# Four extra 64-column products in each score tile of two batches of a decoder layer

## The chip, the cores and the metric

The kernel runs on one core of one Trainium2 chip. The time is the device time of one execution in microseconds (us), the median of several runs. TensorE multiplies matrices, VectorE and ScalarE work element by element, GpSimd does the slower element work and the scattered stores, and SyncE issues most transfers.

## What is computed

One decoder layer over 8 batches of 256 tokens with 128 channels, all in fp32: an attention in which each token looks at 96 chosen keys, a retention over a context, and a mixture of eight experts, each followed by a layer norm. The change lies in the attention. Its core is, cut down:

```python
I = where(local, inf, index_scores); I = where(causal, -inf, I)
_, idx = top_k(I, 96)                      # 64 near keys and 32 far ones
key, value = gathered by idx
scores = (q_c . key_c + q_r . key_r) * scale
attn = softmax(scores)
out = (attn . value) @ W_out
```

## The kernel before

Each batch goes through four stages. Stage a makes queries, keys and the list of far keys; stage b is the attention; stage c the attention's output, the retention and two norms; stage d the router. A last part, the tiles of 128 sorted token rows, runs the experts. The five engines run one program each. `program` writes all of them in the same order: in step n, batch n is in stage b, batch n+1 in stage a, batch n-1 in stage c, batch n-2 in stage d, and each step has `NS` = 20 slots. Expert tiles fill some slots, at the earliest from step 2 on, so the steps of batches 0 and 1 have none. An engine takes its instructions in the order written; semaphores carry the waits between engines.

Stage b takes a batch in `NT` = 16 score tiles of 16 tokens and 8 heads (128 rows). Tiles 0 to 3 (before `T0`) look at near keys alone, the other twelve at far ones too. In slot s TensorE does this, and the text calls it a round:

- `scores(s)`: the products of tile s into bank bS (lines 988 to 994). They wait for VectorE or ScalarE to be done with bS, and the far part for `gs`.
- `gather(s+1)`: one to three 512-column products into bank bG with a one-hot matrix, which pick the far keys of the next tile (line 975). VectorE turns bG into `gs` (line 1668).
- some products of stages a and c, and of the experts.
- behind a wait for `m_out` (ScalarE has emptied bank bM): `weigh(s-2)`, small products of probabilities and values (lines 1018 and 1023), `far_latents(s)`, four small transposes, and `turn(s-1)`, which waits for `s_nrm` and transposes the normed probabilities `ppn` of tile s-1 (line 830, bM<-cst,ppn: two 128-column products in tiles from 4 on, one before).

Beside it VectorE takes the maximum of the scores (`nmx`), divides (`rls`, `ppn`), makes `gs`, and does stage a's search for the largest index scores; ScalarE does the exponential (`pp`) and copies bM into `pts`, `vgs` and `ots`.

Bank bM has 512 columns of 4 bytes: transposed probabilities at 0 to 255, far values at `LATENT` = 256, weighed values at `WEIGHED` = 384 to 447. Columns 448 to 511 are not used in stage b. `ident` is a 128x128 identity held in `cst`; in `MM(out, stationary, moving)` the second argument is loaded into the array and the third streams through.

Of the kernel before, what the change touches and what calls it, by code (L numbers as in the profile page):

```python
# [35 lines left out]
NT = L // TQ  # L36
# [7 lines left out]
SCORES_AT = (5.5, 6, 7, 8, 9.5, 10.5, 11.5, 12.5)  # L44
LEAD_A, LEAD_C, LEAD_D = 2, 2, 4
FIRST_C = -4


def most_tiles(batches):
# [164 lines left out]
def build(nc, io, out):  # L214
    ctx = ExitStack()
    with ctx:
# [124 lines left out]
        bG, bS = pb("bG"), pb("bS")  # L341

        bM = pb("bM")
        TURNED, LATENT, WEIGHED = 0, 256, 384
        bW = [pb("bW0"), pb("bW1")]
        bC = pb("bC")
        bH = pb("bH")
# [79 lines left out]
        def program(stage_a, stage_b, stage_c, stage_d, tile_list, tile, collect, summed, means, normed, dense, dense_end):  # L427

            listed = {GROUPS[g][0][-1] + 2: g for g in range(len(GROUPS))}
            for step in range(-2, NB + 1):  # L430
# [4 lines left out]
                for s in range(NS):  # L435
                    def run(f, at_, k, lead, low=0):

                        for own, i in ((at_ + lead, batch(k)), (at_ + lead - NS, batch(k + 1))):
                            if i is not None and own >= low:
                                if own == low:  # L440
                                    f(low - 1, i)
                                f(own, i)
# [5 lines left out]
                    run(stage_a, s, 1, LEAD_A)  # L448
                    run(stage_c, s, -1, LEAD_C, FIRST_C)
                    run(stage_b, s, 0, 0)  # L450
# [3 lines left out]
                    run(stage_a, s + 0.5, 1, LEAD_A)  # L454
                    run(stage_c, s + 0.5, -1, LEAD_C, FIRST_C)
                    run(stage_d, s + 0.5, -2, LEAD_D)
# [187 lines left out]
        def _(pool):  # L644
# [88 lines left out]
            def stage_c(s, i):  # L733
                oc.batch(-1 if s < FIRST_C else 0, i.n)
                if s == FIRST_C:
                    pool.wait_ge(d_cx[i.par].sem, d_cx[i.par].at(i.half, 32))

                    pool.wait_ge(c_full.sem, c_full.at(i.n - 1, C_AT["state"] + 1))

                    pool.wait_ge(r_q.sem, r_q.at(i.n - 1, 1))  # L740
                    rotate(rkn[:, :, :], cn[:, i.par, :, :], "cos_k", "sin_k", r1, r2, r_k)
                if s == 0:

                    pool.wait_ge(c_av.sem, c_av.at(i.n - 1, 2))
                    pool.sem_inc(s_pass.sem, 1)
                    heads = lambda ap: ap.rearrange("p t (g v e) -> p t g v e", v=4, e=RD)
                    for v in range(4):
                        nc.gpsimd.tensor_copy(heads(cnm[:, :, v, :])[:, :, :, v, :],
                                              heads(cn[:, i.par, :, :])[:, :, :, v, :]).then_inc(r_v.sem, 1)
                if s == 3:  # L750
                    pool.wait_ge(c_x1.sem, c_x1.at(i.n, 1))
                    pool.wait_ge(r_k.sem, r_k.at(i.n, 1))
                    rotate(rqn[:, :, :], x1[:, :, :], "cos_q", "sin_q", r1, r2, r_q)
# [68 lines left out]
        def _(pe):  # L822
            for s_ in (a_full, g_full, s_full, m_full, c_full, c_av, r_full):
                pe.sem_inc(s_.sem, s_.per * s_.lead)
            MM = nc.tensor.matmul
            ident = C("ident")

            def flip(dst, src, n, lo=0):

                return MM(dst, src, ident[lo:lo + n, lo:lo + n], is_transpose=True, start=True, stop=True)  # L830
# [13 lines left out]
            for h in range(NH):  # L844
                lo = 64 * (h % 2)
                last = MM((bM, bC)[h % 2][0:CQ, 32 * (h // 2):32 * (h // 2) + 32], wuqT[lo:lo + 64, h // 2, :], wukvT[lo:lo + 64, h // 2, :],
                          start=True, stop=True)
# [131 lines left out]
            def scores(i, tile):  # L979
                p, g = i.par, tile - T0  # L980
                if tile == 0 or tile > T0:
                    pe.wait_ge(s_max.sem, s_max.at(i.n, tile))
                else:
                    pe.wait_ge(s_exp.sem, s_exp.at(i.n, tile))
                o = 0
                q = qall[:, p, 128 * tile:128 * tile + 128]
                if tile < T0:
                    MM(bS[:, o:o + 96], q, kd[:, p, 0:96], start=True, stop=True).then_inc(s_full.sem, 1)
                    return
                k0 = 32 * ((tile - T0) // 2)  # L990
                MM(bS[:, o:o + 96], q, kd[:, p, k0:k0 + 96], start=True, stop=True, skip_group_check=True)  # L991
                pe.wait_ge(g_out.sem, g_out.at(i.n, g + 1))
                for c in range(4):
                    last = MM(bS[32 * c:32 * c + 32, o + 96:o + SW], qall[0:96, p, 128 * tile + 32 * c:128 * tile + 32 * c + 32],  # L994
                              gs[:, g % 2, 128 * c:128 * c + 128], start=True, stop=True, skip_group_check=True)
                last.then_inc(s_full.sem, 1)

            def far_latents(i, tile):
                g = tile - T0
                for c in range(4):  # L1000
                    o = LATENT + 32 * c
                    flip(bM[:, o:o + 32], gs[0:32, g % 2, 128 * c:128 * c + 128], 32)

            def turn(i, tile):

                pe.wait_ge(s_nrm.sem, s_nrm.at(i.n, tile + 1))
                w = ppn[:, tile % 2, :]
                if tile < T0:
                    return flip(bM[0:96, 0:128], w[:, 0:96], 128)
                flip(bM[:, 0:128], w[:, 0:128], 128)  # L1010
                return flip(bM[:, 128:256], w[:, 96:SW], 128)
# [17 lines left out]
            def stage_b(s, i):  # L1029
                if s < 0:  # L1030
                    return
                if s == 0:
                    pe.wait_ge(a_free.sem, a_free.at(i.n, 15))
                if s == int(s):
                    if s < NT:
                        scores(i, s)
                    if T0 <= s + 1 < NT:
                        gather(i, s + 1)
                    return
                if s > int(s) + 0.25:  # L1040
                    return
                s = int(s)
                if 1 <= s <= NT + 1:
                    pe.wait_ge(m_out.sem, m_out.at(i.n, s - 1))
                    pe.sem_inc(s_pass.sem, 1)
                    if 2 <= s:
                        last = weigh(i, s - 2)
                    if T0 <= s < NT:
                        far_latents(i, s)
                    if s <= NT:  # L1050
                        last = turn(i, s - 1)
                    last.then_inc(m_full.sem, 1)
# [210 lines left out]
            def normed(n):  # L1263
                pass

            program(stage_a, stage_b, stage_c, stage_d, tile_list, tile, collect, summed, means, normed, dense, dense_end)


        @block.scalar
        def _(act):  # L1270
# [144 lines left out]
            def stage_c(s, i):  # L1415
                full = lambda use: act.wait_ge(c_full.sem, c_full.at(i.n, C_AT[use] + 1))
                free = lambda ins: ins.then_inc(c_freeA.sem, 1)
                oc.batch(-1 if s < FIRST_C else 0, i.n)
                if s == 1:
# [87 lines left out]
        def _(dve):  # L1507
# [189 lines left out]
            def stage_c(s, i):  # L1697
# [4 lines left out]
                two = lambda ap: ap.rearrange("p (t c) -> p t c", t=2)  # L1702
                oc.batch(-1 if s < FIRST_C else 0, i.n)
                if s == -2.5:
# [242 lines left out]
```

## Time and profile before

| | |
|---|---|
| runs of before | 773.82, 762.03, 766.42 us; median 766.42 |
| profiled execution | 757.35 us, of which the span from the first to the last instruction is 755.5 |
| instructions | 18822, on TensorE 6549 products and as many weight loads |
| busy, share of the span | TensorE 85%, its weight loads 66%, VectorE 63%, ScalarE 49%, GpSimd 36% |
| mean granted TensorE clock | 0.868 of full speed |

In the profile PE is TensorE's product, PEld its weight load, DVE VectorE, ACT ScalarE, POOL GpSimd. An fp32 product that is no transpose leaves two PE records and two PEld records, a transpose one of each. "128*96 128x512" is a stationary operand of 128 rows and 96 columns and a moving one of 128 rows and 512 columns. PEclk is the clock that was granted to TensorE, as a share of 2.4 GHz: it is either 1.00 or 0.50, and a value between them is a stretch that holds both. Products are pipelined, so that the duration of one record is longer than the time until the next one starts, and a busy share of 100% is not full use. A span of "us" in the timeline covers all records of its row ("x8").

### The profile page before, as it was taken

The page shows a single profiled execution, that of the slowest core. Times are in us where ns is not written, and L with a number is a line of the kernel's source. Part 1 is how long each engine was busy: PE and PEld are TensorE (multiplying, and loading weights), DVE is VectorE, ACT ScalarE, POOL GpSimd, SP SyncE. Part 2 cuts the span into 40 slices and gives each one's busy share as a digit, 9 for nine tenths or more (in the row PEclk, how much of TensorE's full clock was granted, in tenths as well). Part 3 has the DMA queues.
Part 4 walks back from the last instruction along what each step waited for, and adds up shares of the span by engine and source line. Part 5 has one row for each costly group of instructions (what it writes and reads, how often), then busy time and mean ns, then how long its engine had stood idle before and what let it go on. Part 6 is the DMA issues. An engine that isn't in the chain of part 4 may idle for free.

```text
span 755.5 us, 18822 instructions
## 1 busy us (share of the span) xinstructions
PE 644.0 (85%) x6549; PEld 495.8 (66%) x6549; DVE 473.1 (63%) x1733; ACT 369.5 (49%) x1271; POOL 274.7 (36%) x451
## 2 busy tenths in 40 slices
PE   5469988997999899988998999889977997567794
PEld 4245664675577677755686777757766776457794
DVE  1618647876985797578766975687744674314334
ACT  4335445453565476544554766355533643234352
POOL 0345602911840163139701540179622001342053
PEclk9857598897799999965899999968986998669998
DMA  4080030020306330303044416040523222248760
GB/s 150 1 299 2 2 106 1 2 107 1 124 3 204 108 97 19 111 16 129 9 170 127 116 41 195 23 144 17 172 86 101 87 82 64 87 138 267 227 214 26
DMA packets 43413, 73.23 MB, mean 97 GB/s; under 512 B 7664, under 2 KB 31544, under 8 KB 42168
## 3 DMA queue, kind: packets, MB, share of 16 engines
q1 hardware_dynamic: 41528, 68.36, 28.7%
q0 software_dynamic: 1792, 3.67, 1.5%
q8 instruction: 53, 0.87, 0.5%
q14 instruction: 40, 0.33, 0.1%
HBM read 61.69 MB, written 10.32 MB: 95 GB/s over the span
## 4 chain that ended last, share of the span: by engine, by line
PE 44%; issue 10%; POOL 9%; DVE 8%; ACT 3%; DMA 1%; POOLq 0%; DVEq 0%
PE bM L830 6%; PE bG L975 5%; PE bH L1185 5%; PE bR L1202 4%; PE bM L1018 3%; PE bS L994 3%; PE bM L1023 2%; POOL sorted_tokens L780 2%; PE bR L1107 2%; PE bW L1247 2%; PE bS L991 2%; PE bC L830 2%; PE bC L1124 2%; PE bW L1202 1%; PE bC L1075 1%
## 5 line engine op out<-in xcount | busy, mean ns | idle before, releaser
L1385 ACT ACTIVATE pp<-pp,nmx 128x224 f32<-128x224 f32 x96 | 46.4, 483 | 79.5 <-DVE nmx L1662 78.1
L1668 DVE TENSOR_TENSOR gs<-bG,rank_t 96x512 f32<-96x512 f32 x96 | 65.5, 682 | 18.5 <-PE bG L975 18.5
L1467 ACT ACTIVATE ht<-bH,wt 128x128 f32<-128x128 f32 x192 | 54.7, 369 | 39.1 <-PE bH L1185 39.1
L1397 ACT COPY pts<-bM 128x256 f32<-128x256 f32 x96 | 35.4, 369 | 63.0 <-PE bM L830 62.7
L1731 DVE TENSOR_TENSOR sm<-bC,cst 128x512 f32<-128x512 f32 x64 | 43.6, 681 | 34.0 <-PE bC L1124 33.6
L1202 PE MATMUL bR<-wt,ht 128*128 128x128 f32 x328 | 51.1, 305 | 15.8 <-DVE taken L1808 13.3
L726 POOL TENSOR_TENSOR r<-x,cst 128x256 f32<-128x256 f32 x8 | 5.8, 724 | 153.7 <-DVE x L1695 153.7
L975 PE MATMUL bG<-oh,kspl 128*96 128x512 f32 x160 | 61.3, 467 | 0.0
L1202 PEld LDWEIGHTS bR<-wt,ht 128*128 128x128 f32 x328 | 46.9, 215 | 21.2 <-issue 15.1
L1185 PE MATMUL bH<-xt,wt 128*128 128x128 f32 x384 | 56.6, 295 | 4.1 <-DVE xt L1855 2.0
L1650 DVE TENSOR_SCALAR ppn<-pp,rls 128x224 f32<-128x224 f32 (+1 forms) x128 | 49.8, 389 | 14.1 <-DVE rls L1647 0.5
L830 PE MATMUL bM<-cst,ppn 128*128 128x128 f32 (+1 forms) x224 | 56.2, 323 | 0.9 <-DVE ppn L1650 0.9
L1185 PEld LDWEIGHTS bH<-xt,wt 128*128 128x128 f32 x384 | 52.5, 210 | 5.8 <-DVE xt L1855 2.7
L1662 DVE CUSTOM_DVE_ANT_0 pp<-bS,cst 128x224 f32<-128x224 f32 x96 | 36.5, 380 | 29.1 <-PE bS L994 29.1
L1018 PE MATMUL bM<-pts,ckw 96*32 96x64 f32 x512 | 52.6, 293 | 0.3 <-ACT ots L1405 0.3
L1124 PE MATMUL bC<-qV,kS 128*128 128x512 f32 x64 | 37.0, 578 | 13.1 <-DVE sm L1731 10.6
L994 PE MATMUL bS<-gs,qall 96*32 96x128 f32 x768 | 44.7, 308 | 1.0 <-DVE gs L1668 0.2
L780 POOL DMA_INDIRECT sorted_tokens<-x,slot x28 | 29.9, 1068 | 42.7 <-DVE slot L1837 27.5
L1018 PEld LDWEIGHTS bM<-pts,ckw 96*32 96x32 f32 x512 | 19.5, 113 | 39.2 <-issue 38.3
L1023 PEld LDWEIGHTS bM<-pts,vgs 128*32 128x32 f32 x1536 | 44.2, 121 | 0.0
L830 PE MATMUL bM<-cst,gs 32*128 32x32 f32 x384 | 44.0, 236 | 0.0
L1023 PE MATMUL bM<-pts,vgs 128*32 128x16 f32 x1536 | 43.4, 198 | 0.0
(288 smaller groups left out, 1595.9 us busy)
## 6 DMA issues: line engine op xcount, KB each, us to landing
wt<-in_experts SPq DMA_DIRECT2D x64, 578.0 KB, 4.1
sidx<-far_slots SPq DMA_DIRECT2D x8, 1536.0 KB, 7.0
xs<-sorted_tokens SPq DMA_DIRECT2D x56, 64.0 KB, 3.7
expert_rows<-ot SPq DMA_DIRECT2D x56, 64.0 KB, 3.5
sorted_tokens<-acc SPq DMA_DIRECT2D x11, 256.0 KB, 7.8
cst<-shape_constants SPq DMA_DIRECT2D x1, 1603.5 KB, 6.3
xn<-in_x SPq DMA_DIRECT2D x8, 128.0 KB, 4.9
xr<-in_x SPq DMA_DIRECT2D x8, 128.0 KB, 3.2
```

The costliest lines, as they stand in the source:

```text
L830: return MM(dst, src, ident[lo:lo + n, lo:lo + n], is_transpose=True, start=True, stop=True)
L975: last = MM(w[0:96, :], table, oh[:, pair % 2, kt, SLOTS * (tile % 2):SLOTS * (tile % 2) + SLOTS], start=(n == 0), stop=(n == len(products ...
L994: last = MM(bS[32 * c:32 * c + 32, o + 96:o + SW], qall[0:96, p, 128 * tile + 32 * c:128 * tile + 32 * c + 32], gs[:, g % 2, 128 * c:128 * ...
L1018: last = MM(bM[32 * j:32 * j + 32, WEIGHED:WEIGHED + 64], near, pts[0:96, 0:128].rearrange("p (q a b) -> p b a q", a=4, b=2)[:, j, :, :], ...
L1023: last = MM(bM[32 * j:32 * j + 32, WEIGHED:WEIGHED + 64].rearrange("p (a q) -> p a q", a=4)[:, :, 4 * c:4 * c + 4], vgs[:, g % 2, 32 * c:3 ...
L1124: full(MM(w[:, :], kS[:, t, g, :], qV[:, g, :, :], start=True, stop=True))
L1185: last = MM(w[:, 128 * f:128 * f + 128], wt[:, t % NW, 128 * f:128 * f + 128], xt[:, t % 2, :], start=True, stop=True)
L1202: last = MM(w[:, 0:128], ht[:, t % 2, f, :], wt[:, t % NW, W2_AT + 128 * f:W2_AT + 128 * f + 128], start=(f == 0), stop=(f == 3))
L1385: AC(pp[:, s % 2, 0:w], bS[:, 0:w] if s < T0 else pp[:, s % 2, :], ACT.Exp, scale=1.0 if s < T0 else -1.0, bias=nmx[:, s % 2:s % 2 + 1], a ...
L1467: last = AC(ht[:, t % 2, f, :], w[:, 128 * f:128 * f + 128], ACT.Relu, bias=wt[:, t % NW, FF + f:FF + f + 1])
L1650: TS(ppn[:, t % 2, 0:w], pp[:, t % 2, 0:w], rls[:, t % 2:t % 2 + 1], None, ALU.mult).then_inc(s_nrm.sem, 1)
L1668: TT(gs[:, g % 2, :].rearrange("p (t j) -> p t j", j=FAR), bG[0:96, :].rearrange("p (t j) -> p t j", j=FAR), rank_t[:, :].rearrange("p (o ...
```

## The change

Batches 0 and 1 get, in each of their rounds 1 to 16, four products of the identity with its own first 64 columns, written to the unused columns of bM. They stand behind `weigh` and `far_latents` and ahead of `turn`, so that they come after the wait for `m_out` and before the one for `s_nrm`. Their result is read by nobody, and they signal nothing.

```diff
+FIRST_LISTED, FILLERS = 2, 4
...
-        TURNED, LATENT, WEIGHED = 0, 256, 384
+        TURNED, LATENT, WEIGHED, UNUSED = 0, 256, 384, 448
...
                     if T0 <= s < NT:
                         far_latents(i, s)
+                    if i.n < FIRST_LISTED and s <= NT:
+                        for _ in range(FILLERS):
+                            MM(bM[:, UNUSED:UNUSED + 64], ident, ident[:, 0:64], start=True, stop=True, skip_group_check=True)
                     if s <= NT:
                         last = turn(i, s - 1)
                     last.then_inc(m_full.sem, 1)
```

Line numbers of the changed kernel are one higher from the first added line on, and four higher behind the added loop. TensorE's queue in batch 0, a round with far keys before:

```order
L991 MATMUL bS<-kd,qall 128x96
L994 MATMUL bS<-gs,qall 32x128 x4
L975 MATMUL bG<-oh,kspl 96x512 x2
L1018 MATMUL bM<-pts,ckw 32x64 x2
L1023 MATMUL bM<-pts,vgs 32x4x4 x8
L830 MATMUL bM<-cst,gs 128x32 x4
L830 MATMUL bM<-cst,ppn 128x128 x2
```

The same round on TensorE now:

```order
L992 MATMUL bS<-kd,qall 128x96
L995 MATMUL bS<-gs,qall 32x128 x4
L976 MATMUL bG<-oh,kspl 96x512 x2
L1019 MATMUL bM<-pts,ckw 32x64 x2
L1024 MATMUL bM<-pts,vgs 32x4x4 x8
L831 MATMUL bM<-cst,gs 128x32 x4
L1053 MATMUL bM<-cst 128x64 x4
L831 MATMUL bM<-cst,ppn 128x128 x2
```

Four products (L1053) stand ahead of the two transposes of the turn, and nothing else moved. At the start of batch 0, where stage a of batch 1 lies between the first rounds (bW is its bank), TensorE's queue before:

```order
L988 MATMUL bS<-kd,qall 128x96
L830 MATMUL bM<-cst,ppn 96x128
L988 MATMUL bS<-kd,qall 128x96
L1018 MATMUL bM<-pts,ckw 32x64 x2
L830 MATMUL bM<-cst,ppn 96x128
L926 MATMUL bW<-kiT,qiT 64x192 x4
```

And now:

```order
L989 MATMUL bS<-kd,qall 128x96
L1053 MATMUL bM<-cst 128x64 x4
L831 MATMUL bM<-cst,ppn 96x128
L989 MATMUL bS<-kd,qall 128x96
L1019 MATMUL bM<-pts,ckw 32x64 x2
L1053 MATMUL bM<-cst 128x64 x4
L831 MATMUL bM<-cst,ppn 96x128
L927 MATMUL bW<-kiT,qiT 64x192 x4
```

In the first round the group stands right behind the scores, since there is nothing to weigh yet; in the second it delays the turn and stage a's products (L927).

## Rows read from the trace of the kernel before

**Rows 1.** The page: TensorE's busy time, and the granted clock in 40 slices

```profile
PE 644.0 (85%) x6549; PEld 495.8 (66%) x6549; DVE 473.1 (63%) x1733; ACT 369.5 (49%) x1271; POOL 274.7 (36%) x451
...
PEclk9857598897799999965899999968986998669998
```

**Rows 2.** Busy time by stretch of the span, with the columns' names

```profile
core 0: us, PE busy (x) PEld busy (x) DVE busy (x) ACT busy (x) POOL busy (x), PEclk, DMA share, GB/s
49.00:61.30 12.30, 10.93 (x45) 6.86 (x45) 6.99 (x25) 5.46 (x20) 0.00 (x0) 0.50 0.58 220
61.40:71.60 10.20, 9.54 (x102) 6.42 (x101) 8.99 (x38) 5.59 (x26) 6.06 (x13) 1.00 0.01 3
71.60:80.00 8.40, 8.30 (x82) 5.38 (x85) 7.86 (x26) 3.20 (x15) 8.01 (x13) 0.50 0.01 2
80.00:92.00 12.00, 12.00 (x100) 8.04 (x101) 5.54 (x20) 5.49 (x17) 7.87 (x16) 0.50 0.01 1
92.10:105.90 13.80, 13.24 (x209) 9.88 (x205) 8.75 (x26) 7.72 (x26) 0.00 (x0) 1.00 0.46 146
116.00:122.80 6.80, 4.33 (x21) 2.79 (x22) 4.70 (x14) 2.14 (x10) 0.72 (x1) 0.50 0.00 0
122.80:133.00 10.20, 9.69 (x75) 5.74 (x74) 9.59 (x35) 8.06 (x30) 2.66 (x9) 1.00 0.01 2
133.00:139.80 6.80, 6.74 (x73) 4.82 (x74) 6.36 (x26) 2.47 (x12) 6.56 (x10) 0.51 0.01 2
142.50:172.00 29.50, 27.74 (x396) 20.24 (x396) 23.18 (x74) 16.68 (x56) 10.44 (x19) 1.00 0.19 69
283.00:316.60 33.60, 33.58 (x454) 27.05 (x453) 23.49 (x80) 19.97 (x68) 7.64 (x17) 1.00 0.17 57
```

**Rows 3.** Timeline of TensorE: start, duration, engine, line, product; turns and a gather

```profile
52.98 0.42 PE L830 MATMUL bM<-cst,ppn 128*96 128x128 f32 x1
...
78.95 0.69 PE L830 MATMUL bM<-cst,ppn 128*128 128x128 f32 x2
...
82.95 0.47 PE L830 MATMUL bM<-cst,ppn 128*128 128x128 f32 x1
...
99.09 0.44 PE L830 MATMUL bM<-cst,ppn 128*128 128x128 f32 x2
...
100.55 0.39 PE L975 MATMUL bG<-oh,kstk 128*96 128x512 f32 x1
...
101.82 0.44 PE L830 MATMUL bM<-cst,ppn 128*128 128x128 f32 x2
...
105.91 0.44 PE L830 MATMUL bM<-cst,ppn 128*128 128x128 f32 x2
```

**Rows 4.** Timeline and one line's durations (shortest/median/longest): the price of a product

```profile
62.28 0.55 PE L937 MATMUL bW<-wkv,xT 128*128 128x64 f32 x4
...
79.22 0.55 PEld L991 LDWEIGHTS bS<-kd,qall 128*128 128x128 f32 x2
...
99.26 0.30 PEld L991 LDWEIGHTS bS<-kd,qall 128*128 128x128 f32 x2
...
L991 PEld LDWEIGHTS bS<-kd,qall x192: 186/192/338, 63.6 to 623.5; 128*128 128x128 f32 x192
```

**Rows 5.** Timeline of TensorE: waits ahead of an instruction and who ended them

```profile
54.00 0.74 PE L988 MATMUL bS<-kd,qall 128*128 128x96 f32 x2 [0.60 <-ACT pp L1385]
...
71.34 0.50 PE L991 MATMUL bS<-kd,qall 128*128 128x96 f32 x2 [0.44 <-DVE nmx L1662]
...
116.93 0.45 PE L830 MATMUL bC<-cst,rqn 128*128 128x128 f32 x1 [0.97 <-POOL rqn L731]
...
118.92 0.74 PE L988 MATMUL bS<-kd,qall 128*128 128x96 f32 x2 [1.54 <-ACT pp L1385]
```

**Rows 6.** Groups by line, TensorE, ten rounds in batch 3's step: expert products

```profile
L1202 PE MATMUL bR<-wt,ht 128*128 128x128 f32 x32 | 4.3, 278 | 0.0
L1185 PE MATMUL bH<-xt,wt 128*128 128x128 f32 x24 | 3.2, 275 | 0.0
```

## Prediction

> **What bounds the kernel now.** I read four views: the page for the whole, the busy time by stretch for where TensorE's clock stands, the timeline for one score tile's round on TensorE, and the groups by line for what expert work costs in later steps. On the page TensorE is the fullest engine, 644.0 of 755.5 us, and its granted clock dips in several of the 40 slices [rows 1]. The busy time by stretch shows what lies under the two batches that change. Batch 0 is scored from about 50 to 106 us, batch 1 from about 114 to 172. TensorE ran at half speed (1.2 GHz) from 49 to 61.3, from 71.6 to 92, from 116 to 122.8 and from 133 to 139.8, and at full speed (2.4 GHz) between [rows 2]. In all of them but the third it was busy nearly without a break at either speed. So the round of a tile is bound by TensorE in order: 4.00 us from one turn to the next at half speed (78.95 to 82.95), 2.73 us at full speed (99.09 to 101.82) although that round has one gather product more, which took 0.32 us (100.55 to the next row's start at 100.87) [rows 3]. Like for like that is 4.00 against 2.41, a ratio of 0.60. VectorE is a second bound in part: it was busy 8.99 of 10.20 us in 61.4 to 71.6, 7.86 of 8.40 in 71.6 to 80 and 6.36 of 6.80 in 133 to 139.8, but only 5.54 of 12.00 in 80 to 92 [rows 2].
>
> **What is added.** 16 groups of four products in each of two batches, 128 in all; nothing is removed. In fp32 a plain product leaves two records. The nearest row has exactly the added shape, 128x128 stationary and 64 moving columns: four records took 0.55 us at full speed [rows 4]. With some 0.22 us as the last one's own tail that is 0.11 us from start to start. Two 128-column weight loads took 0.30 us at full and 0.55 us at half speed, and one such load lasts 0.19 us as a rule and 0.34 us at the longest [rows 4]; taking off the last load gives 0.11 and 0.21 from start to start. So a group of eight records costs 0.88 us at full and 1.7 us at half speed. All four products load the same stationary operand. Whether a load is then shortened no fp32 row here shows; I take the full price, and half of it, 0.44 us, as the lower bound.
>
> The group stands behind the wait for m_out and the old products of the round, and ahead of the turn, which waits for s_nrm. It adds no wait. Behind it on TensorE's queue are the turn, the next scores and the next gather; ScalarE waits for the turn (the copy to pts), VectorE for the scores and the gathered keys. The write goes to columns 448 to 511 of bM, which nobody reads. What hides a group is TensorE's own idle time in that round, and nothing else.
>
> **Stretch by stretch**, against the profiled execution. The sixteen turns of batch 0 start from 52.98 to 105.91 [rows 3]: two before 61.1, four more to 71.6, four to 92, six after that.
> - 49 to 61.3, half speed, two groups: 3.4 us, of which the wait of 0.60 us for ScalarE at 54.00 [rows 5] takes some: +2.8. Should the denser TensorE work bring the full clock one change earlier, some 3 us at a ratio of 0.60 come back: -1.2, which I take.
> - 61.4 to 71.6, full speed, four groups: 3.5 us. TensorE was idle 0.66 us, partly waiting for VectorE (0.44 us at 71.34) [rows 2, 5], and VectorE was 88% busy, so it sets the pace in half of this: +1.8, between 0 and 2.9.
> - 71.6 to 92, half speed, four groups. This is what the change can win. The fall at 71.6 came when TensorE had waited for VectorE (71.34). With four full-array products in each round TensorE has work in such a wait, and I expect the clock to stay up. Then the first 8.4 us stay bound by VectorE and shrink by 0.4 only, with two groups hidden. The other 12 us become 12 x 0.60 = 7.2, plus two groups of 0.88 = 9.0. Together -3.4.
> - 92.1 to 105.9, full speed, six groups: 5.3 us, less 0.56 us of idle time [rows 2]: +4.7.
> - Batch 1's first group is hidden: TensorE then waits 0.97 and 1.54 us for GpSimd and ScalarE (116.93 and 118.92) [rows 5]. The second falls in the half-speed stretch behind those waits: +1.7. The next three, in 122.8 to 133: 2.6 less 0.51 idle [rows 2] = +2.1. Together +3.8.
> - 133 to 139.8, half speed, one group: VectorE sets the pace, the group is hidden and 0.5 is won if the clock stays up: -0.5.
> - 142.5 to 172, full speed, ten groups: 8.8 us. TensorE was idle 1.76 us here [rows 2]. A check on how much of such work shows in the time: the same ten rounds in the step of batch 3 carry 32 and 24 expert records more [rows 6], at 0.11 us 6.2 us, and last 33.6 against 29.5 us [rows 2], 4.1 us or about two thirds. Between that and 8.8 - 1.8 = 7.0 I take +6.2.
>
> The sum is 2.8 - 1.2 + 1.8 - 3.4 + 4.7 + 3.8 - 0.5 + 6.2 = +14.2 us. The steps follow each other on TensorE, so the delay reaches the end. The profiled execution took 757.35 us (span 755.5 and 1.85 around it), below all three timed runs; their median is 766.42. Against the profiled run the sum gives 771.6, against the median 780.6.
>
> **A rule that speaks against the gain.** From 80 to 92 us TensorE was busy 12.00 of 12.00 us and had the half clock throughout [rows 2]. The Trainium skill, page "TensorE: Matmul & The Clock Gate", section "Why this matters for your kernels", says that keeping the engine busy without idle gaps brings the full clock. The trace disagrees for that stretch; and by that rule products added to an engine that is already never idle would change no clock. The Trainium skill, page "TensorE: Matmul & The Clock Gate", section "Part 4: PE-mode transpose", says that transposes don't count as busy in the same way. The trace neither shows nor excludes it; it would speak for ordinary products like the added ones, and for my -3.4.
>
> **Rivals.**
> - The clock does not answer. For it: the half-speed stretch was already full of TensorE work, and an added group spends as long on loading weights as on streaming. Then the four groups of 71.6 to 92 cost 1.7 each, perhaps 5 us after VectorE's share, in place of -3.4; the group at 136 costs 1.2 in place of -0.5; the early rise (-1.2) is lost. That is 14.2 + 8.4 + 1.7 + 1.2 = +25.5: 792.
> - The groups are mostly hidden: VectorE and the chain around a tile set the pace, as the two thirds of the batch 3 check hint. With half of the positive terms (19.3 us) and the gains kept: 9.7 - 5.1 = +4.6: 771. Against it: TensorE idles only 0.56 us in 13.8 and 1.76 in 29.5 [rows 2].
> - It is faster. At full speed all groups together cost some 19 us net, and each microsecond of half speed that goes gives back 0.4. So the balance turns when 48 us of half speed go. The profile shows 12.3, 20.4, 6.8 and 6.8, 46 in all, in these two batches. The timed median is 9 us above the profiled run; if those 9 us are more half-speed time (some 22 us of it) in these very steps, and the groups hold the clock through all, 68 us go: 19 - 27 = -8: 758. Against it: the stretch at 116 follows tiles that have no groups (rounds 17 on), and the start to 50 us has none either.
> - It does not do what it says only in one way that I can see: the clock of later steps, which hold no added product, shifts by a few microseconds either way because everything arrives later. That widens each case by some 5 us and is in the range.
>
> **How the numbers follow.** Forecast 0.45 (780, from 771 to 788); clock does not answer 0.22 (792, 784 to 800); mostly hidden 0.18 (771, 765 to 777); faster 0.15 (758, 750 to 765). The range that leaves out about one in ten on each side is 760 to 797. The three runs of before spread from 762 to 774, so less than 2% (15 us) is about what can't be told from no change. Below 751 lies a third of the faster case: 0.05. Above 782 lie two fifths of the forecast and nearly all of the first rival, 0.18 + 0.20 = 0.38. Within 2%: 0.57.
>
> **What the changed profile would show.** Right: the four added products take 0.85 to 0.9 us ahead of a turn at full speed; the clock stays at 1.00 from 61 to beyond 100 us; rounds at the end of batch 0 grow from 2.73 to about 3.6 us, and the last turn of batch 1 lies 12 to 16 us later than 171.87. First rival: a row at 0.50 between 70 and 95 us with rounds of over 5 us. Mostly hidden: idle time ahead of turns and scores gone, rounds as long as before. What would make the forecast wrong is above all a weight load that is skipped or overlapped for the repeated stationary operand (group at 0.44 us), and half-speed stretches of other length in the timed runs than in the profiled one.

## The result and the profile after

The changed kernel took 783.87 us (median of 4 runs, 779.01 to 787.09), the kernel before 764.22 us (median of 4, 761.32 to 773.82). The ratio is 1.0257 with a 95% interval of 1.0200 to 1.0314: slower by some 20 us. A second comparison, among the experiments, gave 770.44 against 755.70 us, ratio 1.0206, 1.0152 to 1.0260: slower by 15 us. Ratios are made from runs that were not disturbed, medians from all runs, so that the two can differ.

The page of the changed kernel, TensorE's busy time and its granted clock in 40 slices (19.5 us each), answers to [rows 1]:

```profile
PE 669.0 (86%) x6805; PEld 525.5 (67%) x6805; DVE 474.4 (61%) x1733; ACT 370.8 (47%) x1271; POOL 274.5 (35%) x451
...
PEclk9999997999689999956689999977995999659998
```

TensorE worked 25.0 us more (669.0 against 644.0), and yet its clock digits are higher in batch 0: slices 4 and 5, which were 7 and 5, are 9. The digits of slices 1 to 3 can't be compared, as the rows further down show. The busy time by stretch, the same stretches of the span as in [rows 2]:

```profile
core 0: us, PE busy (x) PEld busy (x) DVE busy (x) ACT busy (x) POOL busy (x), PEclk, DMA share, GB/s
49.00:61.30 12.30, 10.83 (x69) 8.41 (x69) 6.36 (x23) 6.20 (x22) 0.00 (x0) 1.00 0.67 254
61.40:71.60 10.20, 10.20 (x113) 7.48 (x113) 9.35 (x40) 5.72 (x26) 5.97 (x13) 1.00 0.01 3
71.60:80.00 8.40, 8.40 (x109) 6.84 (x108) 7.88 (x28) 3.07 (x13) 8.01 (x13) 1.00 0.01 2
80.00:92.00 12.00, 12.00 (x158) 9.57 (x161) 7.66 (x22) 5.86 (x21) 7.38 (x16) 1.00 0.02 2
92.10:105.90 13.80, 13.53 (x186) 10.74 (x179) 6.25 (x20) 5.79 (x19) 0.00 (x0) 1.00 0.41 145
116.00:122.80 6.80, 4.39 (x27) 3.27 (x28) 4.68 (x16) 1.72 (x8) 2.39 (x4) 0.67 0.01 2
122.80:133.00 10.20, 10.20 (x56) 7.23 (x57) 6.19 (x19) 7.30 (x23) 0.00 (x0) 0.72 0.00 0
133.00:139.80 6.80, 6.80 (x67) 5.05 (x66) 6.63 (x25) 3.21 (x15) 4.90 (x12) 1.00 0.01 2
142.50:172.00 29.50, 29.50 (x408) 23.19 (x409) 19.86 (x66) 15.95 (x47) 14.30 (x25) 1.00 0.22 69
```

From the first turn of batch 0 to its last TensorE now ran at full speed; the stretch from 71.6 to 92 us that had half the clock is gone. But TensorE's idle time is gone as well: 10.20 of 10.20, 13.53 of 13.80 and 29.50 of 29.50 us busy, where it was 9.54, 13.24 and 27.74. Where its clock was full before, TensorE was already the bound, and it now has more to do.

The 1.00 of the first row is not to be trusted as far as 53.5 us. The timeline of TensorE shows it, the same two lines in the changed kernel:

```profile
49.68 1.62 PE L903 MATMUL bW<-xT,iwq 128*128 128x192 f32 x4 [0.55 <-ACT xT L1320]
...
53.53 0.46 PE L989 MATMUL bS<-kd,qall 128*128 128x96 f32 x2
53.83 1.03 PE L1053 MATMUL bM<-cst 128*128 128x64 f32 x8
```

and in the kernel before, whose clock is given as 0.50 there:

```profile
48.53 1.62 PE L902 MATMUL bW<-xT,iwq 128*128 128x192 f32 x4 [0.55 <-ACT xT L1316]
...
52.45 0.74 PE L988 MATMUL bS<-kd,qall 128*128 128x96 f32 x2
```

The first line took 1.62 us in both, so the changed kernel too had half the clock there, and the 1.00 stands for "not recorded". The second took 0.46 against 0.74 us: the clock had risen just ahead of the first group (53.83). The timeline of TensorE in the changed kernel, the same rounds as in [rows 3] and the last turns of batches 0 and 1:

```profile
54.69 0.27 PE L831 MATMUL bM<-cst,ppn 128*96 128x128 f32 x1
...
76.32 0.39 PE L831 MATMUL bM<-cst,ppn 128*128 128x128 f32 x2
...
90.98 0.39 PE L831 MATMUL bM<-cst,ppn 128*128 128x128 f32 x2
...
98.18 1.10 PE L1053 MATMUL bM<-cst 128*128 128x64 f32 x8
99.12 0.39 PE L831 MATMUL bM<-cst,ppn 128*128 128x128 f32 x2
...
101.80 1.10 PE L1053 MATMUL bM<-cst 128*128 128x64 f32 x8
102.74 0.39 PE L831 MATMUL bM<-cst,ppn 128*128 128x128 f32 x2
...
108.58 0.39 PE L831 MATMUL bM<-cst,ppn 128*128 128x128 f32 x2
...
182.94 0.39 PE L831 MATMUL bM<-cst,ppn 128*128 128x128 f32 x2
```

The round that took 2.73 us (99.09 to 101.82) takes 3.62 us (99.12 to 102.74), 0.89 us more; the group itself fills 0.94 us ahead of the turn (98.18 to 99.12, 101.80 to 102.74). Before, the last turn of batch 1 started at 171.87 us; it is now 11.1 us later. Of these, 1.1 us are there ahead of any added product: the first scores of batch 0 start at 51.73 us in place of 50.59. The timeline of the kernel before, the seventh and eleventh turn of batch 0, which answer to 76.32 and 90.98, and this last one:

```profile
74.95 0.69 PE L830 MATMUL bM<-cst,ppn 128*128 128x128 f32 x2
...
92.75 0.44 PE L830 MATMUL bM<-cst,ppn 128*128 128x128 f32 x2
...
171.87 0.44 PE L830 MATMUL bM<-cst,ppn 128*128 128x128 f32 x2
```

From that turn to the end of the span the first profile of before took 583.6 us, that of the changed kernel 598.7, although nothing is added there. This second part of the loss, 15.1 us in the two profiles, is what the runs below had to explain.

### The profile page after: what moved, and what is told of

It reads as the page before. It is cut to its first block, busy times and chain, and to the rows that moved or that the text cites. A ratio compares the mean times of both kernels' runs of the same rounds, so it can differ in the third digit from the quotient of the medians.

```text
span 781.6 us, 19334 instructions
## 1 busy us (share of the span) xinstructions
PE 669.0 (86%) x6805; PEld 525.5 (67%) x6805; DVE 474.4 (61%) x1733; ACT 370.8 (47%) x1271; POOL 274.5 (35%) x451
## 4 chain that ended last, share of the span: by engine, by line
PE 43%; issue 10%; POOL 8%; DVE 7%; ACT 3%; DMA 2%; another core or an unknown queue 1%; POOLq 0%; DVEq 0%
PE bM L831 6%; PE bH L1189 5%; PE bG L976 5%; PE bR L1206 4%; PE bM L1019 3%; PE bS L995 3%; POOL sorted_tokens L781 2%; PE bM L1024 2%; PE bR L1111 2%; PE bS L992 2%; PE bC L831 2%; PE bW L1206 2%; PE bC L1079 1%; DMA gb<-expert_rows,slot 1%; PE bC L1128 1%
## 5 line engine op out<-in xcount | busy, mean ns | idle before, releaser
L1206 PEld LDWEIGHTS bR<-wt,ht 128*128 128x128 f32 x328 | 46.9, 215 | 21.2 <-issue 15.1
L976 PE MATMUL bG<-oh,kspl 128*96 128x512 f32 x160 | 59.3, 454 | 0.0
L1189 PEld LDWEIGHTS bH<-xt,wt 128*128 128x128 f32 x384 | 53.9, 214 | 5.9 <-DVE xt L1859 3.5
L1654 DVE TENSOR_SCALAR ppn<-pp,rls 128x224 f32<-128x224 f32 (+1 forms) x128 | 47.8, 373 | 14.1 <-DVE rls L1651 0.5
L831 PE MATMUL bM<-cst,ppn 128*128 128x128 f32 (+1 forms) x224 | 54.0, 312 | 0.9 <-DVE ppn L1654 0.8
```

The source lines that it names most:

```text
L976: last = MM(w[0:96, :], table, oh[:, pair % 2, kt, SLOTS * (tile % 2):SLOTS * (tile % 2) + SLOTS], start=(n == 0), stop=(n == len(products ...
L1189: last = MM(w[:, 128 * f:128 * f + 128], wt[:, t % NW, 128 * f:128 * f + 128], xt[:, t % 2, :], start=True, stop=True)
L1206: last = MM(w[:, 0:128], ht[:, t % 2, f, :], wt[:, t % NW, W2_AT + 128 * f:W2_AT + 128 * f + 128], start=(f == 0), stop=(f == 3))
L1654: TS(ppn[:, t % 2, 0:w], pp[:, t % 2, 0:w], rls[:, t % 2:t % 2 + 1], None, ALU.mult).then_inc(s_nrm.sem, 1)
```

## The experiments

Twelve runs follow, four on each of three chips; each is one kernel, profiled once and, save for the two of the kernel before, timed several times. Each time below stands against executions of the kernel before on the same chip: 762.76 us on the first chip (25 executions), 757.71 on the second (13), 755.70 on the third (17). Theory A: the loss is the price of the groups in batches 0 and 1, less what a held clock gives back. Theory B: what comes later in the program makes most of it.

**One batch alone.**

```diff
-                    if i.n < FIRST_LISTED and s <= NT:
+                    if i.n == 0 and s <= NT:
```

> The added products stand in batch 0 alone. In the profile of the changed kernel batch 0's rounds, first turn to last, took 53.9 us against 52.9 before: the price of the groups and the held clock nearly cancel. Theory A (direct price, less what the held clock gives back): about +2 to +4 us against the kernel before, ratio 1.003 to 1.005, batch 0 at full speed throughout. Theory B (what comes later in the program, shifted half-speed stretches in steps that hold no added product, makes most of the loss): a loss of +6 to +10 us here too, since the later steps are shifted as well. Theory C (the clock rise in batch 0 was chance): half speed again between 71 and 92 us, and +8 us or more.

Measured: 772.68 us, ratio 1.0107 (1.0060 to 1.0155). And with `i.n == 1`:

> The added products stand in batch 1 alone. In the changed kernel's profile batch 1's sixteen rounds took 63.8 us against 56.2 before. Theory A (direct price): +7 to +9 us, ratio 1.009 to 1.012; with the batch 0 kernel the two losses add up to less than the 19.6 us of the change, and the rest is open. Theory B (later steps shifted): the same +6 to +10 us as with batch 0 alone, so that the two can't be told apart by their sum, but here batch 0 keeps its half-speed stretch from 71 to 92 us.

Measured: 773.52 us, ratio 1.0131 (1.0033 to 1.0229). The two losses, 1.1 and 1.3%, add up to the change's 2.1 to 2.6%. Batch 1's is no more than either theory expected; its profile keeps the half-speed stretch of batch 0 (71.4 to 91.9 us). Batch 0's, +4.6 to +11.8 us by the interval, is above the 2 to 4 us that I expected of theory A and in the range of theory B, while its profile shows batch 0's sixteen rounds (first turn to last) at 53.9 us, just as in the changed kernel. So this run did not decide, and spoke against me if anything.

**The early groups of batch 0 alone.**

```diff
+                    if i.n == 0 and s <= 8:
```

> The groups stand in batch 0's rounds 1 to 8 alone, 32 products. Theory A: the clock fell at 71.6 us since TensorE did little full-array work there; with the groups it stays up, and rounds 9 to 16 run at full speed without them, as they did before from 92 us on. The eight late groups, nearly all uncovered at 0.88 us, are saved: 6 to 8 us below the kernel with all of batch 0's groups, and 3 to 6 us faster than the kernel before. Theory C (the groups themselves must go on to hold the clock): half speed returns soon after round 8, and the time is that of the kernel before or 3 us above it.

Measured: 765.64 us, ratio 0.9997 (0.9948 to 1.0045). The rows of this kernel's stretches:

```profile
71.60:80.00 8.40, 8.40 (x112) 6.49 (x110) 7.48 (x27) 3.33 (x14) 8.01 (x14) 1.00 0.01 2
80.00:92.00 12.00, 12.00 (x171) 8.93 (x170) 8.74 (x26) 8.07 (x24) 8.34 (x14) 1.00 0.23 64
92.00:100.50 8.50, 7.94 (x128) 5.78 (x128) 5.09 (x16) 4.55 (x17) 0.00 (x0) 1.00 0.44 147
```

The clock stayed full through batch 0, behind round 8 too, where there are no groups: theory C falls. The sixteen rounds took 46.8 us, 7.1 less than with all groups, as 8 x 0.88 = 7.0 has it, and 6.2 less than in the first profile of before. But the 3 to 6 us that I expected to win do not arrive in the timed runs. Against the kernel with all of batch 0's groups (both on one chip) the timed time fell by 7.0 us as expected; against the kernel before it is the same, give or take 4 us. Batch 1, which has no groups here, ran at full speed from 117.2 us, between its second turn and its third, to its last:

```profile
117.30:164.40 47.10, 44.23 (x582) 30.79 (x580) 40.43 (x137) 29.23 (x101) 22.45 (x40) 1.00 0.14 44
```

With all of batch 0's groups and none in batch 1 it did so from 128 us on. That the half-speed stretch of 133 to 139.8 us goes is therefore not shown to be the work of batch 1's own groups.

**Transposes in place of products.**

```diff
-                            MM(bM[:, UNUSED:UNUSED + 64], ident, ident[:, 0:64], start=True, stop=True, skip_group_check=True)
+                            flip(bM[:, UNUSED:UNUSED + 64], ident[0:64, :], 64)
```

> As in the change, 128 added operations in both batches, but each is a transpose of the identity's first 64 rows into the same 64 columns, in place of a plain product: one record in place of two, so half the price, 0.44 us a group. Nothing of the reference's computation changes. Theory A with transposes counting as work for the clock: batch 0 stays at full speed, and the loss falls from 19.6 to some 5 to 10 us. If transposes don't count: half speed again from 71 to 92 us, and the loss is 10 to 16 us, since half-priced groups are added to a slow stretch.

Measured: 763.65 us, ratio 1.0004 (0.9951 to 1.0056), below both expectations. A group by itself took what was expected, here from 97.97 to the turn at 98.36 in the timeline of this kernel's TensorE:

```profile
97.97 0.46 PE L831 MATMUL bM<-cst 64*128 64x64 f32 x4
98.36 0.44 PE L831 MATMUL bM<-cst,ppn 128*128 128x128 f32 x2
```

And its busy time by stretch:

```profile
71.60:92.00 20.40, 19.64 (x266) 13.94 (x266) 17.47 (x54) 10.06 (x36) 17.88 (x28) 1.00 0.12 34
```

0.39 us a group where I expected 0.44 and a plain one takes 0.89, and the clock was full from 71.6 to 92. So in this profile the clock was held with transposes too. The sixteen rounds of batch 0 took 48.8 us. At less than half price the loss is gone, to within 4 us either way; a gain is not shown.

**The kernel before, profiled twice more** (no edit).

> The kernel before, profiled once more. From the first turn of batch 3 to the end its first profile took 498.7 us (256.8 to 755.5); five kernels that add nothing there took 503.7 to 512.2 us. Theory D (the first profile of before was a short one, and the later steps don't depend on the change): 502 to 508 us now. Theory B (added products make the later steps longer): 497 to 501 us again.

> The kernel before, profiled a third time, with the same two expectations: 502 to 508 us from the first turn of batch 3 to the end by theory D, 497 to 501 by theory B. Also the length of the half-speed stretch in batch 0, some 20 us in the first profile: if it is as long here, what the held clock gives back is as the first profile says; if it is shorter, the gain from holding the clock is smaller.

Measured: 757.53 and 764.62 us, span 755.7 and 762.8. From the first turn of batch 3 they took 500.1 and 495.6 us, below theory D's 502 to 508 and near theory B's 497 to 501. But two kernels with groups on the same chip took as little (next), which is against B; the later part differs between the chips. What the two profiles showed beside it: the half-speed stretch of batch 0 is not the same in each execution.

Its stretch in the second profile, in the busy time by stretch:

```profile
77.30:91.00 13.70, 13.56 (x111) 9.04 (x111) 8.21 (x25) 6.27 (x19) 9.57 (x20) 0.50 0.02 2
```

And in the third:

```profile
75.60:102.90 27.30, 27.24 (x237) 18.68 (x238) 14.88 (x45) 11.86 (x36) 12.74 (x23) 0.50 0.24 74
```

13.7 and 27.3 us at half speed, after 20.5 in the first profile; batch 0's rounds took 50.9, 57.2 and 52.9 us. What there is to win in batch 0 swings by 6 us from one execution to the next.

**Thin products.**

```diff
+                            MM(bM[:, UNUSED:UNUSED + 64], ident[0:32, :], ident[0:32, 0:64], start=True, stop=True, skip_group_check=True)
```

> As in the change, but the 128 products have 32 rows in place of 128 (the first 32 rows of the identity as stationary and moving operand): the same columns to load and to stream, and the same two records each, so the same price of 0.88 us a group, with a quarter of the array's rows at work. If the clock is held by the array's rows at work, the half-speed stretches of batch 0 return and the time is that of the change plus 3 to 8 us, 787 to 792. If it is held by instructions or columns whatever their rows, the time is that of the change, 780 to 785, with batch 0 at full speed.

Measured: 807.21 us (790.51 to 811.07, four executions), 49.5 us above the kernel before; the fastest of the four is still 33 us above it. The first direction holds, the size is off by far. The profile is of the slowest of the four, but all four had a low clock, 0.84 to 0.86 on the mean, where the changed kernel's eight had 0.87 to 0.89. The busy time by stretch:

```profile
57.40:145.00 87.60, 87.04 (x615) 66.17 (x615) 34.47 (x119) 26.24 (x92) 19.55 (x40) 0.50 0.08 24
145.00:170.00 25.00, 23.03 (x109) 17.84 (x108) 10.37 (x37) 8.36 (x28) 2.39 (x4) 0.50 0.00 1
```

The durations (shortest, median, longest) of the added weight loads in this kernel:

```profile
L1053 PEld LDWEIGHTS bM<-cst x256: 180/328/366, 54.1 to 229.0; 32*128 32x128 f32 x128
```

And in the changed kernel:

```profile
L1053 PEld LDWEIGHTS bM<-cst x256: 186/192/338, 53.7 to 182.8; 128*128 128x128 f32 x128
```

TensorE was busy all but without a break through batch 0's rounds (the first row), and had half the clock from 57 to 170 us. It had been full from about 54 us, so that it fell with the first groups. The median weight load lasted 328 ns in place of 192, the half-speed duration. The added products not only failed to hold the clock, they kept it down: batch 0's rounds took 90.1 us. The price is the same in columns and records, so what differs is the rows of the array at work. This kernel's later part, from the first turn of batch 3, took 491.4 us with all 128 products ahead of it: theory B is wrong on this chip.

**Two products in a group.**

```diff
-FIRST_LISTED, FILLERS = 2, 4
+FIRST_LISTED, FILLERS = 2, 2
```

> Two products in each group in place of four, in the same places. Theory A (direct price of 0.11 us a record, less what the held clock gives back): half the price, so about +8 to +10 us against before in place of +20 if the clock is still held, ratio 1.010 to 1.013. If two products are too few to hold it: half speed again from about 71 to 92 us and +12 to +15 us.

Measured: 758.31 us, ratio 1.0070 (0.9998 to 1.0141). Its upper half is theory A's +8; the median is but 0.6 us above before's. Batch 0's rounds took 50.2 us, with the clock full until 100 us. It fell at 100.2 us, where groups of four kept it up. The later part took 495.8 us. The interval holds half of the change's loss (1.010) as well as none, so that nothing is shown on how the price goes with the number.

**The changed kernel again** (no edit).

> The changed kernel once more, on the chip of the next three. Theory A (the loss is the price of the groups in batches 0 and 1, less what the held clock gives back): from the first turn of batch 3 to the end it takes no longer than the kernel before does on average, 495 to 506 us, where its first profile had 512.2; the timed ratio lies between 1.013 and 1.026. Theory B (the later steps get longer with the added products): 508 to 514 us again.

Measured: 770.44 us, ratio 1.0206 (1.0152 to 1.0260). From the first turn of batch 3: 500.7 us, so the 512.2 us of its first profile do not always come with the change. The last turn of batch 1 started at 181.8 us.

**The late groups alone.**

```diff
+                    if i.n < FIRST_LISTED and 9 <= s <= NT:
```

> Groups of four in rounds 9 to 16 of both batches alone, 16 groups in place of 32. These rounds ran mostly at full speed and without idle time on TensorE before, so nothing hides the groups and little clock is to be won. Theory A: 16 groups of 0.88 us, +12 to +15 us against the kernel before, ratio 1.016 to 1.020, most of the loss of the change with half of its products, and the half-speed stretch that begins between 70 and 77 us in batch 0 is still there. If the loss were spread evenly over the groups: half of it, +7 to +10 us.

Measured: 770.38 us (764.54 to 783.81), ratio 1.0169 (1.0117 to 1.0220). Half of the groups make some four fifths of the loss of all by the ratios (1.69 against 2.06%) and all of it by the medians (14.7 us both), as theory A has it; the interval just reaches the 1.013 of an evenly spread loss. Its profile is of the slowest of its four executions and shows what else can happen. The busy time by stretch:

```profile
54.00:77.90 23.90, 21.03 (x176) 12.35 (x175) 19.54 (x72) 11.64 (x52) 10.13 (x19) 1.00 0.13 49
77.90:149.60 71.70, 68.11 (x494) 53.30 (x488) 27.06 (x89) 21.46 (x72) 14.23 (x26) 0.50 0.08 29
```

The 1.00 of the first row is again not a record as far as 64.3 us: the products took their half-speed times until then. The clock fell at 77.9 us as without any groups, and then the eight groups of batch 0, full-array products, did not raise it again. They began at 84.4 us; the last turn behind them started at 128.3, with the clock still at half, and it came back at 149.6 us, ahead of batch 1's groups. A group took 1.76 us there (97.92 to 99.68), as the timeline of TensorE shows:

```profile
97.92 1.97 PE L1053 MATMUL bM<-cst 128*128 128x64 f32 x8
99.68 0.64 PE L831 MATMUL bM<-cst,ppn 128*128 128x128 f32 x2
```

**Both where it pays.**

```diff
+                    if (i.n == 0 and s <= 8) or (i.n == 1 and 4 <= s <= 7):
```

> Groups of four where TensorE waits for VectorE or where the clock fell: rounds 1 to 8 of batch 0 and 4 to 7 of batch 1, 12 groups. Theory A: batch 0's rounds, first turn to last, take 46 to 48 us as with the eight early groups alone, against 51 to 57 before; batch 1's stay at 54 to 57 with no half-speed stretch in rounds 5 to 8, where three profiles of before have one. Against the kernel before: 0 to -8 us, ratio 0.990 to 1.000. If the clock falls as soon as the groups end, in rounds 9 to 16: ratio 1.003 or more.

Measured: ratio 0.9945 (0.9886 to 1.0003), while the median of all 12 runs is 758.81 us (744.21 to 769.40), 3.1 us above before's. The ratio rests on three of the twelve executions. The two point different ways, so it is not shown to beat the kernel before. In its profile batch 0's rounds took 50.0 us, not the 46 to 48 that I expected, because the clock was still at half when its first groups came. The timeline of its first and third group:

```profile
54.10 1.86 PE L1053 MATMUL bM<-cst 128*128 128x64 f32 x8
...
64.72 1.11 PE L1053 MATMUL bM<-cst 128*128 128x64 f32 x8
```

Batch 1's rounds took 56.7 us, without a half-speed stretch in rounds 5 to 8; but so did the kernels without groups in batch 1, above.

**Eight products in a group.**

```diff
-FIRST_LISTED, FILLERS = 2, 4
+FIRST_LISTED, FILLERS = 2, 8
```

> Eight products in each group in place of four, in the same places. The clock is held already by four, so that nothing more is won and the whole of the added price shows: 128 products of 0.22 us are 28 us more than the change, and the waits that hid part of its groups are used up. Theory A: +22 to +28 us beyond the change, ratio 1.05 to 1.06 against the kernel before, a group of sixteen records 1.8 us. If the loss had come from somewhere else than the price of the products (their place ahead of the turn, a wait), it would not double: ratio 1.03 to 1.04.

Measured: 798.53 us (794.93 to 814.84), ratio 1.0543 (1.0486 to 1.0600), 28.1 us above the changed kernel on the same chip by the medians, 25 by the two ratios: 0.20 to 0.22 us for each of the second 128 products. In its profile, at full speed, a group of sixteen records took 1.84 us (99.35 to 101.19), and from the eleventh turn to the last 22.1 us passed (119.42 to 141.49) where the changed kernel took 17.6: 0.89 us for each of five doubled groups, nothing hidden, as theory A has it. Its profile is of one of the two slowest of its five executions; the busy time by stretch:

```profile
56.00:98.90 42.90, 42.26 (x241) 32.84 (x240) 16.59 (x63) 11.38 (x45) 19.05 (x40) 0.50 0.01 1
98.90:141.50 42.60, 41.95 (x520) 35.64 (x516) 17.91 (x58) 14.08 (x48) 0.00 (x0) 1.00 0.15 48
```

Here the clock was at half when the groups began, at 53.0 us, and stayed there for 45.9 us, with the double groups in every round.

The turns' starts in the profiles, read from the timeline as shown above, and the spans, all in us:

```
profile           batch 0: first, last turn   batch 1: last turn   span    from there to the end
before                 53.0   105.9                171.9           755.5        583.6
before, second         53.8   104.8                170.7           755.7        585.0
before, third          53.1   110.3                180.7           762.8        582.1
changed                54.7   108.6                182.9           781.6        598.7
changed, again         53.7   107.6                181.8           768.9        587.1
batch 0 only           54.2   108.0                172.4           770.9        598.5
batch 1 only           53.0   105.9                180.3           770.6        590.3
batch 0, early         53.8   100.5                164.4           761.1        596.7
as transposes          54.4   103.2                170.3           761.3        591.0
thin                   55.2   145.3                229.4           809.3        579.9
two                    53.3   103.6                178.1           760.3        582.2
late only              54.1   128.3                203.2           782.0        578.8
both, early            55.8   105.7                172.1           755.3        583.2
eight                  56.3   141.5                230.4           810.8        580.4
```

The last column is 590 to 599 us in the four profiles of the first chip (batch 0 only to as transposes) and 579 to 587 in the eight of the other two, with added products (578.8 to 587.1) and without (582.1 and 585.0) alike. So on the second and third chip what comes behind batch 1 does not depend on the groups. On the first chip this is not shown. The kernel before was not profiled there; its timed runs were 5 to 7 us longer there than on the other two, less than the column's difference. The busy time by stretch from the last turn of batch 1 to the end, in the changed kernel's first profile, with batch 0's groups alone, and with batch 1's alone:

```profile
182.94:781.60 598.66, 516.19 (x5244) 407.68 (x5243) 371.96 (x1365) 287.83 (x1003) 211.88 (x327) 0.87 0.33 101
172.37:770.90 598.53, 518.69 (x5247) 410.10 (x5242) 371.00 (x1365) 288.15 (x1004) 212.48 (x327) 0.86 0.33 101
180.34:770.60 590.26, 507.75 (x5244) 401.37 (x5243) 373.15 (x1365) 287.83 (x1003) 212.09 (x327) 0.88 0.34 103
```

The two longest had the lower clock, 0.87 and 0.86, where the three profiles of before had 0.88 to 0.89. Part of the difference is therefore half-speed time in steps that hold no group.

Taken together, the profiles show where the groups do hold the clock. In the five without groups in rounds 1 to 8 of batch 0 (the three of before, batch 1 only, late only) it fell between 71.4 and 77.9 us. In the five with four plain products in each of these rounds, and the clock full by 65 us, it stayed full until behind batch 0's last turn.

## Why the prediction was right, and where it was off

The forecast was 780 us, slower by about 14, and 783.87 and 770.44 us were measured, slower by 20 and 15. The mechanism was right: a price of 0.89 us a group where TensorE is the bound, less what a held clock gives back. That the sum came so near is in part luck, since it put the whole loss into batches 0 and 1, where the profiles show less of it (below). By its own steps:

- **The price, 0.88 us a group at full speed and 1.7 at half**, was right: 0.89 us by the round (99.12 to 102.74 against [rows 3]), 1.76 us in the late groups' profile, and 25 to 28 us for 128 more products in the run with eight. The lower bound of 0.44 us for a load that is saved did not apply: every added product has its weight loads.
- **The clock stays up from 71.6 to 92 us, -3.4 us**, was right: from the seventh turn to the eleventh it took 17.8 us before (74.95 to 92.75) and takes 14.7 (76.32 to 90.98), -3.1 us.
- **49 to 61.3, +2.8, and the early rise, -1.2 us**: a wrong reason for a real gain. From the first turn to the third 8.2 us became 6.7, where I had summed +1.6. The clock had risen before the first group. In the profiles it rose either between 52 and 54 us, always ahead of the first group, or between 61 and 65, with groups (both early) and without; with eight only at 98.9. Why is open; the groups did not do it. Against the kernel before's second profile, which had the early rise too and took 6.6 us, the two groups cost 0.1 us. They lie in a wait for ScalarE: the one for `rb` (58.41 us there, 58.40 here) was 1.76 us and is 0.65.
- **61.4 to 71.6, +1.8**: rounds three to seven grew from 13.8 to 14.9 us, +1.2, and by 1.7 against the second profile of before (13.2 us), whose clock was full there throughout.
- **The six late groups of batch 0, +4.7**: from the eleventh turn to the last, which holds five of them, 13.2 us became 17.6, +4.4, or 0.89 us each. Nothing was hidden, where I had taken off 0.56 us of idle time.
- **Batch 1, +3.8, -0.5 and +6.2**: its rounds took 56.2 us and take 63.8, +7.6 for 9.5 forecast. From the seventh turn to the last, nine groups, it is +5.5 of the 8.0 that they cost, about two thirds, as the check by batch 3 had it.
- **The sum**: at the last turn of batch 1 the changed kernel was 11.1 us behind by the two first profiles, 14.2 forecast, and 1.1 of the 11.1 lie ahead of the first group. The term that was off most is the start of batch 0. The three profiles of before differ more than that: by this turn the changed kernel (182.9 and 181.8 us) is between 1 and 12 us behind them (170.7, 171.9 and 180.7).
- **"The steps follow each other on TensorE, so the delay reaches the end"** held on the second and third chip, as the last column of the table shows. The first profile of the changed kernel lost another 15 us there, which the sum has at nothing, and the second one 2 to 5. So the last rival's point, that the clock of later steps may shift either way, is not refuted, and some of the 15 to 20 us may come from there.
- **The rivals.** "The clock does not answer" was the case in single executions, where the clock was down before the groups came (late groups, eight), not in the two profiles of the changed kernel. "Mostly hidden" fell with the run of eight. "It is faster" fell; a clock held through all of batch 0 came true and did not suffice.
- **Why the clock stays up.** My reason was that TensorE has work in its waits. The thin products fill the same waits and it fell, so work in the wait is not enough.

**What stays open.** Batch 0's groups alone cost 8 us in timed runs (interval 4.6 to 11.8), while the profiles of before put batch 0's rounds at 50.9 to 57.2 us and that kernel's at 53.9. The one profile on that chip whose batch 0 has no groups (batch 1 only) puts them at 52.9, with its half-speed stretch of 20.5 us. So the later part, with its lower clock, is the likelier place, but no profile of before was taken there. For the same reason it is open why the early groups, with batch 0 at 46.8 us, are no faster in timed runs.

**The rule of the Trainium skill** that was weighed, page "TensorE: Matmul & The Clock Gate", section "Why this matters for your kernels", to keep the engine busy without idle gaps: with the thin products TensorE was busy 87.04 of 87.60 us, with eight products in a group 42.26 of 42.90, and both had half the clock throughout. The trace disagrees again, and more plainly. What the same Trainium skill, that page's section "Part 4: PE-mode transpose", says, that transposes don't count as busy in the same way, was not seen in the run with transposes: the clock held in its profile as with plain products. One profile does not show that the transposes did it.

## What to carry to other kernels

Extra products that keep TensorE's clock up can pay only in rounds where TensorE waits or where the clock would fall; in a round that TensorE bounds at full speed each one costs its whole 0.22 us, and about half of this change's groups stood in such rounds. No placing of them was shown to beat the kernel before. Read from the windows how long TensorE is idle at full clock in each stretch before adding work, and take several profiles of the kernel before: the half-speed stretch that was to be won lasted 13.7, 20.5 and 27.3 us in three executions. Products of 32 rows did not hold the clock where those of 128 rows did, and groups that came with the clock already down did not bring it back for 44 and 46 us. And check a granted clock of 1.00 at the start of a profile against the durations of known products: it can stand for "not recorded".

## What the runs showed of the hardware

- Same columns, same number of records, 32 rows in place of 128: half the clock for 113 us (57 to 170) with TensorE busy 110 of them, +50 us by the median (+33 in the fastest execution) in place of +15 to +20. One profile; all four executions had a mean clock of 0.84 to 0.86.
- Holding and raising are different things. Groups of four full-array products kept a full clock through batch 0 in five of five profiles in which it was full by 65 us; once it was down, four in a round (84.4 to 128.3 us) or eight (53.0 to 98.9) did not bring it back for 44 and 46 us, one profile each. In a third (both, early) it came back 10 us after the first group, at 64.3, no earlier than without groups.
- The part of the program behind batch 1, the same in all kernels, took 590 to 599 us on one chip and 579 to 587 on two others.
